# Newton steps of a layer norm moved from VectorE to GpSimd, its normalisation to ScalarE, key preparation cut into halves, and one small VectorE subtraction moved up by one place

## What is computed

```
h      = layer_norm(x)                          # mean and variance over 256
q_r    = ((h @ Wq.T per head) @ w_kc_q) @ W_qr   # 64 numbers per head and row
k      = rope(ctx)                               # 1601 x 64, per batch
scores = q_r . (k @ W_kr)                        # per head: 256 x 1601
attn   = softmax(scores);  c = attn @ k          # per head: 256 x 64
x      = x + (c @ w_kc_kv per head) @ Wo.T
y      = layer_norm(x)                           # the one that this change touches
gate   = sigmoid(y @ gate_w + gate_b)
t      = feed-forward chain on the last row of each batch (4 steps of norm, d1, gelu, d2)
out    = x + layer_norm(y + gate * broadcast(t))
```

## Time and profile before

| what | value |
|---|---|
| time, median of 3 runs | 1251.82 us (1250.95 to 1254.65) |
| the profiled execution, its own time | 1251.29 us |
| its span (first to last instruction) | 1249.5 us |
| TensorE busy | 1127.6 us, 90% |
| VectorE busy | 925.3 us, 74% |
| GpSimd busy | 874.9 us, 70% |
| ScalarE busy | 662.1 us, 53% |
| mean granted TensorE clock | 0.942 |

### The profile page before, as it was taken

One profiled execution on the slowest core, in us unless ns is written; L12 is line 12 of the kernel. 1 busy time (PEld: TensorE's weight loads), 2 busy tenths in 40 slices (PEclk: granted clock), 3 DMA queues, 4 the chain that ended last, 5 costly groups with the idle time before them and its releaser, 6 DMA issues.

```text
span 1249.5 us, 39647 instructions
## 1 busy us (share of the span) xinstructions
PE 1127.6 (90%) x14852; PEld 742.6 (59%) x14852; DVE 925.3 (74%) x1675; ACT 662.1 (53%) x1163; POOL 874.9 (70%) x796
## 2 busy tenths in 40 slices
PE   5889999989998998989998999989998999999462
PEld 4536666656665665656664665656664666667340
DVE  4378778786869676786869677786869678787548
ACT  1546566545654565545654565545654566466232
POOL 1148977776777876776777876776777877677383
PEclk9999999989998999989998999989998999999655
DMA  9020001000100000000100001000100002000001
GB/s 336 25 67 15 15 15 28 14 15 10 31 11 14 15 15 26 13 15 9 30 12 14 15 15 28 11 15 11 30 11 14 15 18 80 10 17 5 2 2 67
DMA packets 41287, 34.68 MB, mean 28 GB/s; under 512 B 7608, under 2 KB 38648, under 8 KB 40640
## 3 DMA queue, kind: packets, MB, share of 16 engines
q1 hardware_dynamic: 40512, 27.79, 7.9%
q10 hardware_dynamic: 576, 4.19, 0.9%
HBM read 17.27 MB, written 2.10 MB: 15 GB/s over the span
## 4 chain that ended last, share of the span: by engine, by line
PE 76%; DVE 13%; issue 7%; DMA 2%; ACT 1%; POOL 1%; SPq 1%; DVEq 0%; ACTq 0%
PE ps_s L704 12%; PE ps_s L703 12%; PE ps_m L574 12%; PE ps_o L622 7%; PE ps_o L625 7%; PE ps_o L632 7%; PE ps_x L562 4%; DVE mx L896 3%; PE ps_x L648 3%; DVE big L925 2%; PE ps_x L585 2%; DVE sq L963 1%; PE ps_x L509 1%; PE ps_x L508 1%; PE ps_x L675 1%
## 5 line engine op out<-in xcount | busy, mean ns | idle before, releaser
L202 POOL TENSOR_TENSOR plo_all<-big 128x512 f16<-128x512 f32 x640 | 690.0, 1096 | 290.2 <-ACT big L436 289.8
L896 DVE TENSOR_REDUCE mx<-ps_m 128x1 f32<-128x512 f32 (+1 forms) x832 | 547.7, 666 | 237.1 <-PE ps_m L574 211.7
L436 ACT ACTIVATE big<-ps_s 128x512 f32<-128x512 f32 x768 | 458.6, 597 | 392.8 <-PE ps_s L704 391.8
L574 PE MATMUL ps_m<-k_hi,qq 128*128 128x512 f16 x768 | 297.3, 388 | 32.7 <-DVE mx L896 30.1
L703 PE MATMUL ps_s<-qq,k_hi 128*128 128x512 f16 (+1 forms) x832 | 319.1, 384 | 6.1 <-issue 5.7
L704 PE MATMUL ps_s<-qq,k_lo 96*128 96x512 f16 (+1 forms) x832 | 321.2, 386 | 0.0
L622 PEld LDWEIGHTS ps_o<-k,big 128*128 128x128 bf16 x3072 | 187.3, 99 | 121.7 <-issue 5.9
L625 PE MATMUL ps_o<-k,big 128*128 128x64 f16 x3072 | 221.7, 194 | 0.0
L622 PE MATMUL ps_o<-k,big 128*128 128x65 f16 x3072 | 220.6, 194 | 0.0
L632 PE MATMUL ps_o<-k,plo_all 128*128 128x65 f16 x3072 | 220.0, 194 | 0.0
L574 PEld LDWEIGHTS ps_m<-k_hi,qq 128*128 128x128 f16 x768 | 76.6, 100 | 139.0 <-DVE mx L896 47.6
(11 more groups left out here) (196 smaller groups left out, 1033.5 us busy)
## 6 DMA issues: line engine op xcount, KB each, us to landing
qq<-q_hi SPq DMA_DIRECT2D x256, 32.0 KB, 1.9
qq<-q_lo SPq DMA_DIRECT2D x128, 32.0 KB, 1.9
tables<-kv_dram SPq DMA_DIRECT2D x8, 384.0 KB
big<-wq_dram ACTq DMA_DIRECT2D x1, 2048.0 KB, 15.6
xs<-x_dram SPq DMA_DIRECT2D x4, 512.0 KB, 18.1
big<-wo_t_dram SPq DMA_DIRECT2D x1, 2048.0 KB, 13.0
tables<-d_w_dram SPq DMA_DIRECT2D x2, 1024.0 KB, 6.8
out_dram<-big SPq DMA_DIRECT2D x8, 256.0 KB, 2.2
```

The lines of the kernel that those rows point to most:

```text
L202: eng.tensor_tensor(probs_lo(t)[0:r, :], probs(t)[0:r, :], probs_hi(t)[0:r, :], ALU.subtract).then_inc(done, 1)
L436: act.activation(probs(t)[0:r, :], ps_s[0:r, (p * KT + t) % 2, :], ACT.Exp, scale=1.0 / SC).then_inc(p_done, 1)
L574: mm = pe.matmul(ps_m[:, j % 3, :], qq[p % 4][:, 0, a:a + 128], k_hi[par][:, c:c + 512], start=True, stop=True)
L896: dve.tensor_reduce(o, i, AX.X, ALU.max).then_inc(mx_read, 1)
```

## The change

Six things change. (1) The three seed instructions of the root move from pair 2, t = 8 to the end of `post_v` at t = 2. (2) The Newton rounds leave VectorE for GpSimd, as 4 + 4 + 6 `tensor_tensor` instructions of 128x2 (`newton`) at pair 3, behind its tiles 1, 6 and 10; constants 1.5 and -1 come from a small tile. The last two make -mean times the root. (3) The normalisation leaves VectorE for ScalarE (`normalise_u`): two copies of 128x2 and two activations of 128x256 at pair 4, t = 3. (4) Each of the six key instructions is cut into 8 and 5 tiles, and the twelve are laid singly behind low parts of the pairs 0 to 4. (5) The turning of the first key part moves from pair 4, t = 12 to pair 3, t = 12, `transpose_u` the other way. (6) `ctx_low` moves ahead of the maximum that VectorE reads at t = 10. `LO_D` is `(2, 9)` before and after.

```diff
-PREP_OPS = 6
+HALVES = (slice(0, 8), slice(8, KT))
+PREP_OPS = 12
+KEY_SLOTS = {(0, 8): 0, (0, 12): 1, (1, 6): 2, (1, 12): 3, (2, 6): 4, (2, 12): 5,
+             (3, 4): 6, (3, 12): 7, (4, 3): 8, (4, 5): 9, (4, 8): 10, (4, 12): 11}
+ROOT_SLOTS = {(3, 1): 0, (3, 6): 1, (3, 10): 2}
-POST_OPS = 11
-ROOT_OPS = 12
-ROOT_STEPS = {8: 0, 10: 1, 11: 2, 12: 3}
+POST_OPS = 9
+ROOT_OPS = 17
...
+            def newton(m, i):
+
+                o = m * ROOT_OPS + 3 + 4 * i
+                ops = (
+                    (sq[:, :], rs[:, :], rs[:, :], ALU.mult),
+                    (sq[:, :], sq[:, :], hv[:, :], ALU.mult),
+                    (sq[:, :], sq[:, :], consts[:, 0, :], ALU.add),
+                    (rs[:, :], rs[:, :], sq[:, :], ALU.mult),
+                    (nmu[:, :], mv[:, :, 0], consts[:, 1, :], ALU.mult),
+                    (nmu[:, :], nmu[:, :], rs[:, :], ALU.mult),
+                )
+                for k in range(6 if i == 2 else 4):
+                    pool.wait_ge(root, o + k)
+                    pool.tensor_tensor(*ops[k]).then_inc(root, 1)
...
-                    if not last(n):
-                        for k in when.get(p, ()):
-                            keys(n + 1, 1 - par, k)
+                        if not last(n) and (p, t) in KEY_SLOTS:
+                            keys(n + 1, 1 - par, KEY_SLOTS[p, t])
+                        if not first(n) and (p, t) in ROOT_SLOTS:
+                            newton(n - 1, ROOT_SLOTS[p, t])
...
-                        if t == 12 and not last(n) and p in (4, 6):
-                            copy_keys(n + 1, 1 - par, 0 if p == 4 else 3)
+                        if t == 12 and not last(n) and p in (3, 6):
+                            copy_keys(n + 1, 1 - par, 0 if p == 3 else 3)
...
-                            if p == 3 and t == 12:
+                            if p == 4 and t == 3:
+                                normalise_u(n - 1)
+                            if p == 4 and t == 12:
                                 copy_ut(n - 1)
...
+            def normalise_u(m):
+                act.wait_ge(root, m * ROOT_OPS + ROOT_OPS)
+                for all_, one in ((rs_all, rs), (nm_all, nmu)):
+                    copy(all_[:, bass.ds(m * ST, ST)], one[:, :]).then_inc(kept, 1)
+                act.wait_ge(x_saved, m + 1)
+                for st in range(ST):
+                    act.activation(u[:, st, :], u[:, st, :], ACT.Identity, bias=nmu[:, st:st + 1],
+                                   scale=rs[:, st:st + 1]).then_inc(post, 1)
...
             for k in range(2 + K_STEPS):
+                if k == 1:
+                    normalise_u(B - 1)
                 act.wait_ge(var8, k + 1)
...
+                        if t == KT - EARLY and started:
+                            ctx_low(par if p else 1 - par, (p - 1) % NP, g - 1)
                         if t >= KT - EARLY and not (last(n) and p >= NP - 2):
                             read_maxima(p, g + 2, t - (KT - EARLY))
...
-                        if t == 10 and started:
-                            ctx_low(par if p else 1 - par, (p - 1) % NP, g - 1)
...
-                            if p == 2 and t in ROOT_STEPS:
-                                post_root(n - 1, ROOT_STEPS[t])
-                            if p == 3 and t == 8:
-                                post_b(n - 1)
...
-                if k == 0:
-                    for i in range(4):
-                        post_root(B - 1, i)
-                    post_b(B - 1)
```

More of the change, by code:

```diff
@@ L102, in build_xattn_ffn @@
         ve, hv, sq, rs = (sb(k, [128, ST]) for k in ("ve", "hv", "sq", "rs"))
-        mean_all = sb("mean_all", [128, B * ST])
+        nmu = sb("nmu", [128, ST])
+        consts = sb("consts", [128, 2, ST])
+        nm_all = sb("nm_all", [128, B * ST])
         rs_all = sb("rs_all", [128, B * ST])
@@ L163, in build_xattn_ffn @@
         dw_high, dw_low = sem("dw_high"), sem("dw_low")
-        proj_done, post, root, x_saved = (sem(s) for s in ("proj_done", "post", "root", "x_saved"))
+        proj_done, post, root, x_saved, kept = (sem(s) for s in ("proj_done", "post", "root", "x_saved", "kept"))
         ut_done, ut_copied, gate_done, gate_out = (sem(s) for s in ("ut_done", "ut_copied", "gate_done", "gate_out"))
@@ L316, in batch @@
                         make_low(pool, t, lo_p)
-                    if not last(n):
-                        for k in when.get(p, ()):
-                            keys(n + 1, 1 - par, k)
+                        if not last(n) and (p, t) in KEY_SLOTS:
+                            keys(n + 1, 1 - par, KEY_SLOTS[p, t])
+                        if not first(n) and (p, t) in ROOT_SLOTS:
+                            newton(n - 1, ROOT_SLOTS[p, t])
             batches(pool, batch)
             pool.wait_ge(pv_done, B * TB)
+            for i in range(3):
+                newton(B - 1, i)
+            pool.wait_ge(kept, 2 * B)
+            pool.wait_ge(x_saved, B)
             pool.wait_ge(post, B * POST_OPS - 1)
-            pool.wait_ge(x_saved, B)
             for i in range(B * ST):
-                pool.tensor_scalar(u_all[:, i * DM:(i + 1) * DM], xs[:, i * DM:(i + 1) * DM], mean_all[:, i:i + 1],
-                                   rs_all[:, i:i + 1], ALU.subtract, ALU.mult).then_inc(u_ready, 1)
+                pool.tensor_scalar(u_all[:, i * DM:(i + 1) * DM], xs[:, i * DM:(i + 1) * DM], rs_all[:, i:i + 1],
+                                   nm_all[:, i:i + 1], ALU.mult, ALU.add).then_inc(u_ready, 1)
             pool.wait_ge(u_ready, B * ST)
@@ L501, in keys_turned @@
             def keys_turned(n, par, i, psum=ps_xh):
-                pe.wait_ge(prep, n * PREP_OPS + PREP_OPS)
+                pe.wait_ge(prep, n * PREP_OPS + (6 if i % 2 == 0 else 12))
                 for t in range(8) if i % 2 == 0 else range(8, KT):
@@ L732, in batch @@
                                 project(1 - par, (0,))
-                            elif p == 3 and not first(n):
+                            elif p == 4 and not first(n):
                                 take_x((ut_copied, m + 1))
@@ L736, in batch @@
                             elif p == 5 and not first(n):
-                                take_x((post, m * POST_OPS + 11))
+                                take_x((post, m * POST_OPS + 9))
                                 gate_mm(m)
-                            elif p in (4, 6) and not last(n):
-                                i = 0 if p == 4 else 3
+                            elif p in (3, 6) and not last(n):
+                                i = 0 if p == 3 else 3
                                 take_x((kt_copied, n * 4 + (4 + i + 1)))
@@ L832, in _ @@
                 pad(qq[i][64:96, 1, :], 0.0)
+            pad(consts[:, 0, :], 1.5)
+            pad(consts[:, 1, :], -1.0)
             dve.wait_ge(in_small, 16)
@@ L945, in post_v @@
                 dve.tensor_scalar(ve[:, :], mv[:, :, 1], 1e-5, None, ALU.add).then_inc(post, 1)
[L947 to L980 removed]
+                dve.wait_ge(post, o + 6)
+                dve.tensor_scalar(rs[:, :].bitcast(I32), ve[:, :].bitcast(I32), 1, None, ALU.arith_shift_right).then_inc(root, 1)
+                dve.tensor_scalar(hv[:, :], ve[:, :], -0.5, None, ALU.mult).then_inc(root, 1)
+                dve.wait_ge(root, m * ROOT_OPS + 2)
+                dve.tensor_scalar(rs[:, :].bitcast(I32), rs[:, :].bitcast(I32), -1.0, float(0x5F3759DF), ALU.mult,
+                                  ALU.add).then_inc(root, 1)
             def post_c(m, psum):
```

53 lines of the change are left out of this document (12 added, 41 removed).

## The result

The changed kernel takes 1194.97 us (median of 4 runs, 1192.87 to 1200.32), the kernel before, on the same chip, 1252.02 us (4 runs, 1250.95 to 1254.65). The ratio is 0.9548, 95% interval 0.9511 to 0.9585: 57 us less, where 1195.5 us was forecast. The profiled execution took 1192.9 us with a span of 1191.1 us; the mean granted clock rose from 0.942 to 0.961.

What follows compares the result with a forecast made beforehand. TensorE, busy 90% of the span, was taken as the bound, idling in pair 3 and at `max_row`. Terms -49.5 - 10.4 + 2.8 + 1.4 - 0.3 = -56.0 us gave 1195.3, called 1195.5 us; range 1188 to 1207, the forecast's own 1190 to 1201.

Steps and rivals of the forecast that it cites:

- Newton rounds and normalisation off VectorE: Pairs 3 and 4: with nothing of VectorE's between the maxima, pair 3's loss goes; -49.5 us, batch 7 included.
- until the GpSimd instruction beside them is over: Pair 3: VectorE's small instructions sit that long, the maxima queue behind them and TensorE idles; some 7.9 us lost per batch.
- `ctx_low`, -10.4: One place earlier, ahead of a reduction, it no longer delays `max_row`: 0.17 us in 61 places.
- Seeds, +2.8: Pair 2, t = 2: three more small instructions lengthen TensorE's wait for `ctx_m` by 0.4 us in seven batches.
- ScalarE's normalisation, +1.4: Pair 4, t = 3: four new activations delay tile 4's exponential by 0.85 us, leaving up to 0.2 us stall per batch.
- Newton on GpSimd, 3.7 us for fourteen: Pair 3: about 0.19 us each, 0.26 us with the wait on its predecessor, covered by GpSimd's idle time.
- Tail, -0.3: End of kernel: `hp` regains 2.0 us, the second square root behind `normalise_u` comes 1.6 us late.
- Start, 0: Start of kernel: six more fixed parts delay first keys by 1.1 us, but the first half is released earlier; nothing.
- Sum: All terms together -56.0 us, from 1251.3 to 1195.3 us, called 1195.5.
- Keys in halves, 0: Pairs 0 to 4: six more fixed parts, 1.1 us per batch, fall in GpSimd's idle time; nothing.
- Clock near 0.98: Whole kernel: a sign of being right was a mean clock near 0.98.

Runs made afterwards that it cites:

- moving the keys away: The kernel before, with the first four key instructions, uncut, one pair earlier and Newton rounds left in place: 1220.86 us, ratio 0.9737.
- whole keys: The changed kernel with the six key instructions uncut, each alone in a slot of pairs 0 to 3: 1207.71 us, ratio 0.9645.
- a shift: The changed kernel with uncut keys, plus two idle VectorE reductions ahead of tile 2's low part in pairs 2 and 3 of batch 0: 1210.33 us, ratio 0.9653.
- a gap forced: The changed kernel with uncut keys, GpSimd waiting once for VectorE's low part in pairs 2 and 3 of batch 0: 1195.53 us, ratio 0.9530.

## Why the prediction was right, step by step

- **Newton rounds and normalisation off VectorE, -49.5.** Right. Pairs 3 and 4 of six batches went from 242.0 to 191.9 us, of which 2.0 us are `ctx_low`'s twelve places: -48.2 against -47.5. In batch 7 the two took 31.7 us before and take 29.2 now, -2.2 without `ctx_low` against -2.0. The step counted the change as one; the runs divide it: moving the keys away is worth 33 us by itself, the chain another 15 (by difference).
- **VectorE's instruction "until the GpSimd instruction beside them is over".** Right in kind, too short for the largest. The Newton instruction of 2.88 us asked at 528.36, during a low part of GpSimd's that ran from 528.28 to 529.32, and sat over that and the key instruction behind it, whose 1.93 us alone can't make 2.88. It did so in all six batches (2.87 or 2.88 us each). So the wait over more than one instruction, which the experiments ran into, was in the first trace already.
- **`ctx_low`, -10.4.** Right: 0.17 us in every pair, and 8 to 11 us between runs.
- **Seeds, +2.8.** Wrong in size: nothing. The wait for `ctx_m` stayed 0.23 us. The prediction's lower bound had named the reason, and chose the value between: in batch 3 the low part of tile 2 takes 0.49 us less and gives back the 0.4 us that the seeds take.
- **ScalarE's normalisation, +1.4.** Wrong in size: nothing. The exponential is late, as worked out, but TensorE's steps don't grow, so it had more slack than was reckoned.
- **Newton on GpSimd, 3.7 us for fourteen.** Right: 0.19 to 0.20 us at a pitch of 0.27; in the tail 4.0 us from the first to the last.
- **Tail, -0.3.** It is +0.5. The chain was right (square root late, `hp` early), the late part dearer: 1.84 us of VectorE's idle time instead of 1.6.
- **Start, 0.** It is 2.1 us later. But the first score matmul starts anywhere from 77.6 to 80.7 us in the ten experiments, at 77.6 and 79.5 us in two kernels with whole keys that don't differ there, so it isn't the halves that can be blamed.
- **Sum.** The loop gave 61.0 us where the terms had 55.7; the start and the tail took back 2.6 of that. The total was hit partly because these misses cancel.
- **Keys in halves, 0.** Right in size for the wrong comparison. It cost nothing; but the text judged it by the longest piece between two low parts, while what it bought was protection from a wait over a whole run of pieces.
- **Clock near 0.98.** It is 0.961. Pair 3 lost 0.14 to 0.22 of some 23 us in six batches, 24 us of clock time out of the 72 that 0.058 of 1249.5 us make. Of the rest, 40 us lie in the tail, whose clock is 0.56 before and 0.57 after; the change doesn't touch it. Without pair 3's share 48 of 1191 us are left, 0.959. That sum could have been done beforehand.

The Trainium skill (SBUF — State Buffer, "Who interferes with whom") has VectorE and GpSimd block each other for the length of the instruction that came first. The waits of one instruction agree with it: 0.60 us for the variance, 0.96 for a seed. The 2.88, 4.01 and 8.15 us, over two, four and eight GpSimd instructions, are longer than that allows: there the measurement decides, and the one who waits isn't always next.

## What stays open

Why one change between two GpSimd instructions lets VectorE in and another doesn't. The moment of the request (0.31 or 0.47 us into the instruction) isn't it, nor the length of the run alone, since low parts also got in with up to twelve changes of an unbroken run ahead of them. That the whole keys are met by the long wait only in batch 0 isn't explained either. Nor is the chain's 15 us shown by a run of its own. The 2.6 to 4.2 us that TensorE idles at each of the two turns of the hardware loop ("issue") vary from run to run and were not tried.

## What to carry to other kernels

Look on the timeline for tiny instructions with long durations: they are waiting inside, not working, and what is queued behind them pays. Before cutting the other engine's work into pieces, try to move it away from the place where the two meet: one line took away two thirds of pair 3's loss. Where two engines share something and one runs without a gap, give it a wait on the other's result, if the other is what the bound engine waits for.

## What the hardware showed that I had not expected

- A VectorE instruction can be kept out over a whole unbroken run of GpSimd's: 8.15 and 7.92 us for one of 0.68 us, repeated at 8.00 us after a shift, 2.27 us with a gap forced; and 4.0 us for a 128x2 one of 0.15 us.
- On GpSimd a two-scalar instruction on 128x256 float32 numbers takes 0.55 us with multiply and add, 1.21 us as soon as one of the two is a subtraction.
- A GpSimd instruction on two input tiles of 128x2 numbers takes 0.19 us. A line through two forms over two hundred times as large had given the same.
